# Next batch's tokens: rows serve statistics alone, a second copy laid out by feature is centred and scaled, and no row is transposed

## The chip, the cores and the metric

The kernel runs on one core of a Trainium2 chip. The metric is device time in microseconds (us) of one execution, the median of several runs.

## The reference

Input x is 4 batches of 1024 tokens by 1024 features in float32. One block of a pre-norm network is computed:

```
h   = x + attention(layernorm(x))          # 16 heads of 64, block-local window of 256 keys,
                                           # and 64 chosen query tokens per head attend to all 1024 keys
out = h + layernorm(h) @ (W_ffn * scale[:, None]).T + bias
layernorm(x) = (x - mean(x)) / sqrt(var(x) + 1e-5)     # over the 1024 features of a token
```

The chosen tokens are the first, the last, and the 62 with the largest query norm. Their rows of the attention output replace the local ones.

## The kernel before

Every fp32 matmul operand is split into a rounded high part and the rest (`_hi`, `_lo`), and three products are summed. So each product costs three matmul passes, and each operand a copy (ACT, high part) and a subtraction (DVE, low part).

`xT_hi`, `xT_lo` hold a batch's normalised tokens transposed: features on the partitions, 8 groups of 128 features by 1024 tokens. Four batches run one after another. A batch begins with a query phase: 8 slices of 128 query columns are projected, turned back to token rows, stored in memory, and their norms ranked on DVE (`top_find`, `top_rows`, first half of the heads). Then come 8 units of `attend(n, hp)`, one for each pair of heads. Within a unit PE runs the local scores in 4 steps, their transposes, the products with V, the global part, and, between these, the projection of V and K of the next pair in 8 parts (`part(0)` to `part(7)`, L648). In unit 7 these parts are the first query projections of the next batch. The order of all engines is written out by hand; every engine executes its own list in order and waits on semaphores.

**How the next batch's xT is made, before.** The rows of the next batch (for the last batch: of W_ffn, whose "norm" is the scale alone) come one tile of 128 tokens at a time into the slot of `q_store` that the unit's query has just left (`load_rows`, L236). In each unit DVE takes the moments of the tile (`row_moments`, L1066, two `bn_stats`), a chain of 14 links for 1/sqrt by Newton steps and two more for the weight case (`row_roots`, L1073), and normalises into `xn_row` (`row_normalise`, L1076). In the next unit PE transposes the tile in two halves of four 128x128 transposes (`turn_row`, L498; they stand behind `weigh(u, 0)` and `part(2)`), ACT copies each half out of PSUM (`keep_row`, L776), and in units 6 and 7, as xT comes free, ACT and DVE split the kept tiles into `xT_hi` (`row_hi`) and `xT_lo` (`row_lo`).

**SP, the DMA queue.** It issues the loads and the stores in one order. In a unit `hp`: `load_rows` (waits for `q_split`), then `stores` (L245): the next V slice of the weights into `w_raw[0]`, the outputs of steps 0 and 1 (`store_ctx`, 128 KB each), the next K slice into `w_raw[1]`, the outputs of steps 2 and 3.

**POOL.** In a unit (`unit`, L388): `split_key`, `normalise` of steps 0, 1, 2, `split_value`, `normalise` of step 3. `normalise(n, hp, s)` writes one of two output buffers and so waits until the store of step `s - 2` has landed:

```
pool.wait_ge(ctx_stored[s % 2], u * (16 * STEPS // 2) + 16 * (s // 2) + 16)     # L353
```

`split_value(n, hp)` makes `w_hi[0]`, `w_lo[0]` of the V slice of pair `hp + 2`. It waits for that slice in `w_raw[0]` and for PE's end of `part(5)`, and PE waits for it ahead of `part(0)` of unit `hp + 1` (L480).

**The K hand-over.** PE's `part(6)` of the K projection waits until the K half before it has left PSUM: ACT writes `kT_hi` (`k_hi_out`), DVE `kT_lo` (`k_lo_out`, L1125). In `attend` on DVE, `k_lo_out(n, hp + 1, 0)` stands behind `global_maxima`, `row_moments`, `pv_sums(u, 3)`, `top_norms(5)` and `split_q`.

Of the kernel before, what the change touches and what calls it, by code (L numbers as in the profile page):

```python
# [24 lines left out]
P = 128  # L25
# [13 lines left out]
MISC = 4  # L39
# [14 lines left out]
def build(nc, rows_in, wstream, bq, bk, bv, scale_ffn, bias_ffn, out):  # L54
    q_rows = nc.dram_tensor("q_rows", (SEQ * HEADS, HD), F32, kind="Internal").ap()
    ctx_rows = nc.dram_tensor("ctx_rows", (ROWS, HD), F32, kind="Internal").ap()
    idx_dram = nc.dram_tensor("idx_dram", (BATCH, 2 * HEADS * TOPK), U32, kind="Internal").ap()
# [4 lines left out]
    with ExitStack() as ctx:  # L62
# [8 lines left out]
        q_store = sb("q_store", [P, TILES + 2, SEQ])  # L71
# [14 lines left out]
        x_norm = sb("x_norm", [P, 2, HID])  # L86
        ident = sb("ident", [P, P])
        bq_c, bk_c, bv_c = sb("bq_c", [P, PAIRS]), sb("bk_c", [P, PAIRS]), sb("bv_c", [P, PAIRS])
        scale_c = sb("scale_c", [P, KC])
# [5 lines left out]
        ln_scale = sb("ln_scale", [P, 1])  # L95
        is_weight, zero_c = sb("is_weight", [P, 1], U32), sb("zero_c", [P, 1])
        norms = sb("norms", [P, TILES, HEADS])
        norm_rows = x_norm[0:HALF_HEADS, :, :]
        last_rows, xn_row = q_store[:, 0, :], q_store[:, TILES + 1, :]
        x_buf = [last_rows, xn_row]  # L100
# [19 lines left out]
        lin_c, lin_h = q_store[:, 1:3, :], q_store[:, 3:5, :]  # L120
        lin_hb, lin_o = q_store[:, 5:7, :], q_store[:, 7:9, :]
# [17 lines left out]
        rows_loaded = sem("rows_loaded")  # L139
        weight_set = sem("weight_set")  # L140
        ln_step = sem("ln_step"); xn_set = sem("xn_set")
        x_turned = sem("x_turned"); row_out = sem("row_out")
# [71 lines left out]
        def _(sp):  # L214
            for b in range(2):
                sp.sem_inc(q_stored[b], 16)
                sp.sem_inc(o_stored[b], 16)
            for t in range(TILES):
                if t >= 4:
                    sp.wait_ge(first_in[t % 4], 16)  # L220
                sp.dma_start(q_store[:, t + 1, :], rows_in[t]).then_inc(first_in[t % 4], 16)
                if t == 1:
                    for dst, src in ((bq_c, bq), (bk_c, bk), (bv_c, bv), (scale_c, scale_ffn)):
                        sp.dma_start(dst[:, :], src).then_inc(const_in, 16)
# [11 lines left out]
            def load_rows(n, hp):  # L236

                sp.wait_ge(q_split, n * PAIRS + hp + 1)
                apart(sp)
                sp.wait_ge(rows_loaded, n * (16 * TILES) + 16 * hp + 16)  # L240
                apart(sp)
                sp.dma_start(q_store[:, bass.ds(hp + 1, 1), :].rearrange("p a c -> p (a c)"),
                             rows_in[n * TILES + hp + TILES]).then_inc(rows_loaded, 16)
# [1207 lines left out]
```

## Time and profile before

| | |
|---|---|
| median of 3 runs | 2351.7 us (2348.31 to 2351.74) |
| the profiled execution | 2351.89 us |
| its span, first to last instruction | 2350.3 us |
| mean granted TensorE clock | 0.975 |
| busy: PE, DVE, ACT, POOL | 94%, 66%, 36%, 25% |
| chain that ended last | PE 72%, DVE 18%, issue 7%, ACT 2% |

The busy shares are of the span. "Granted clock" is a share of 2.4 GHz; 0.50 is 1.2 GHz. The chain is followed back from the last instruction to whatever released each step; "issue" is time in which the engine waited for nothing that the profile shows. A row of the timeline begins with its start and its duration in us, then engine, line, operation, output and inputs, a count, and in brackets the idle time ahead of it with the engine that ended it. Matmuls overlap, so the cost of a group on PE is read from its start to the next group's start.

### The profile page before, as it was taken

Reading aid. Unit: us, or ns where it says so; the run is one execution under the profiler, and the core shown is the slowest. Engines: PE = TensorE matmul, PEld = TensorE weight load, DVE = VectorE, ACT = ScalarE, POOL = GpSimd, SP = SyncE. Lnnn points to the kernel's source line nnn. Section 1 sums busy time; section 2 is a strip of 40 time slices with the busy share of each in tenths; the row PEclk is TensorE's granted clock in tenths of the full one; section 3 lists DMA queues with packets and bytes.
Section 4 is the critical chain, followed back from the end, with each engine's and each line's share of the span. In section 5 each row is a group of like instructions: output and inputs, shape, how many; then the busy total and the mean of one; then the engine's idle time right before and its main releaser. Section 6 shows DMA issues by size and latency. Waiting matters only on the chain.

```text
span 2350.3 us, 40763 instructions
## 1 busy us (share of the span) xinstructions
PE 2218.1 (94%) x13024; PEld 1879.8 (80%) x13024; DVE 1553.2 (66%) x3434; ACT 857.4 (36%) x2218; POOL 597.6 (25%) x464
## 2 busy tenths in 40 slices
PE   5999989999999899999998999999999987999999
PEld 4878878877788788777887887878887876888887
DVE  5677775664877755748777656486776666666664
ACT  2334445442254344522544355324543551000000
POOL 1231231123321221242312312423123202222221
PEclk9999999999999999999999999999999988999999
DMA  3321111103211111033111111221111103333331
GB/s 126 103 62 51 41 55 38 49 28 107 74 39 49 56 38 49 30 92 87 39 49 41 56 38 39 90 82 48 48 40 51 36 12 125 134 134 134 134 134 72
DMA packets 106170, 159.13 MB, mean 68 GB/s; under 512 B 9616, under 2 KB 75222, under 8 KB 106064
## 3 DMA queue, kind: packets, MB, share of 16 engines
q1 hardware_dynamic: 98128, 138.98, 18.2%
q10 hardware_dynamic: 4608, 16.78, 1.8%
q0 software_dynamic: 3328, 2.17, 0.4%
q8 instruction: 41, 0.67, 0.1%
q14 instruction: 65, 0.53, 0.1%
HBM read 106.48 MB, written 51.41 MB: 67 GB/s over the span
## 4 chain that ended last, share of the span: by engine, by line
PE 72%; DVE 18%; issue 7%; ACT 2%; DVEq 1%; DMA 0%; ACTq 0%; SPq 0%; another core or an unknown queue 0%
PE proj L460 32%; PE proj L742 15%; PE pv L596 7%; PE turn L586 5%; PE score L571 4%; PE pv L640 2%; PE score L621 2%; DVE x_norm L1147 2%; DVE top_idx L1145 2%; DVE top_val L1143 2%; DVE neg_max L1201 2%; PE misc L608 1%; PE misc L508 1%; PE turn L733 1%; DVE kT_lo L1128 1%
## 5 line engine op out<-in xcount | busy, mean ns | idle before, releaser
L460 PE MATMUL proj<-xT_hi,w_hi 128*128 128x512 f32 x1536 | 418.8, 416 | 51.8 <-DVE kT_lo L1128 51.8
L460 PE MATMUL proj<-xT_hi,w_lo 128*128 128x512 f32 x1536 | 413.2, 400 | 0.0
L460 PE MATMUL proj<-xT_lo,w_hi 128*128 128x512 f32 x1536 | 382.1, 391 | 0.0
L460 PEld LDWEIGHTS proj<-xT_hi,w_hi 128*128 128x128 f32 x1536 | 285.7, 196 | 119.5 <-DVE kT_lo L1128 60.9
L460 PEld LDWEIGHTS proj<-xT_lo,w_hi 128*128 128x128 f32 x1536 | 288.4, 188 | 63.3
L460 PEld LDWEIGHTS proj<-xT_hi,w_lo 128*128 128x128 f32 x1536 | 285.2, 191 | 64.4 <-issue 0.7
L864 ACT ACTIVATE probs<-score,neg_max 128x256 f32<-128x256 f32 (+1 forms) x512 | 229.2, 460 | 173.7 <-DVE neg_max L1192 101.5
L354 POOL TENSOR_TENSOR ctx_out<-pv_sum,row_inv 128x256 f32<-128x256 f32 x128 | 82.0, 641 | 755.1 <-DVE pv_sum L1229 749.1
L330 POOL CAST w_hi<-w_raw 128x1024 fp32r<-128x1024 f32 x96 | 111.9, 1166 | 544.4 <-PE proj L460 421.9
L332 POOL TENSOR_TENSOR w_lo<-w_raw,w_hi 128x1024 fp32r<-128x1024 f32 x96 | 237.5, 2474 | 7.8
L596 PE MATMUL pv<-v_nat,pT_lo 128*128 128x128 f32 x1024 | 199.1, 276 | 0.0
L596 PE MATMUL pv<-v_nat,pT_hi 128*128 128x128 f32 x1024 | 196.9, 274 | 1.6 <-DVE pT_lo L1208 1.6
L1208 DVE TENSOR_TENSOR pT_lo<-turn,pT_hi 128x512 fp32r<-128x512 f32 x256 | 165.0, 684 | 42.1 <-ACT pT_hi L877 39.5
L1229 DVE TENSOR_TENSOR pv_sum<-pv,pv_lo 128x256 f32<-128x256 f32 x128 | 54.3, 424 | 193.7 <-ACT pv_lo L888 193.7
L596 PEld LDWEIGHTS pv<-v_nat,pT_hi 128*128 128x128 f32 x1024 | 160.6, 192 | 10.1 <-DVE pv_sum L1229 1.4
L596 PEld LDWEIGHTS pv<-v_nat,pT_lo 128*128 128x128 f32 x1024 | 156.1, 193 | 0.0
L440 POOL TENSOR_TENSOR q_store<-q_store,bias_b 128x1024 f32<-128x1024 f32 x32 | 76.7, 2397 | 287.2 <-DVE q_store L1400 284.8
L877 ACT CAST pT_hi<-turn 128x512 fp32r<-128x512 f32 x256 | 138.9, 595 | 7.2 <-PE turn L586 2.4
L586 PE MATMUL turn<-ident,probs 128*128 128x128 f32 (+1 forms) x1024 | 139.0, 281 | 0.0
L844 ACT ACTIVATE kT_hi<-proj,bk_c 128x512 fp32r<-128x512 f32 x64 | 44.3, 693 | 205.7 <-PE proj L460 205.7
L586 PEld LDWEIGHTS turn<-ident,probs 128*128 128x128 f32 (+1 forms) x1024 | 117.6, 141 | 0.1
L1110 DVE TENSOR_TENSOR q_sq<-q_nat 128x512 f32<-128x512 f32 x64 | 57.1, 892 | 90.5 <-ACT q_nat L814 84.1
(147 smaller groups left out, 3652.9 us busy)
## 6 DMA issues: line engine op xcount, KB each, us to landing
w_raw<-in_wstream SPq DMA_DIRECT2D x96, 512.0 KB, 4.1
q_store<-in_rows SPq DMA_DIRECT2D x72, 512.0 KB, 3.3
q_rows<-q_nat SPq DMA_DIRECT2D x64, 256.0 KB
ctx_rows<-ctx_out SPq DMA_DIRECT2D x128, 128.0 KB, 1.8
q_store<-ctx_rows SPq DMA_DIRECT2D x32, 512.0 KB, 4.1
out<-q_store ACTq DMA_DIRECT2D x32, 512.0 KB, 2.6
bias_b<-in_bias_ffn SPq DMA_DIRECT2D x1, 512.0 KB, 8.0
idx_cols<-idx_dram POOLq DMA_DIRECT2D x32, 1.0 KB, 3.3
```

The source lines that it names most:

```text
L330: pool.tensor_copy(w_hi[b][:, :], w_raw[b][:, :]).then_inc(w_hi_set, 1)
L332: pool.tensor_tensor(w_lo[b][:, :], w_raw[b][:, :], w_hi[b][:, :].bitcast(F32), ALU.subtract).then_inc(w_split[b], 1)
L354: pool.tensor_tensor(ctx_out[:, s % 2].rearrange("p b h d -> p h b d"), pv_sum[:, s % 2].rearrange("p (h b) d -> p h b d", h=2), row_inv[: ...
L440: pool.tensor_tensor(lin_hb[:, b, :], lin_h[:, b, :], bias_b[:, :], ALU.add).then_inc(hb_set, 1)
L460: mm = pe.matmul(proj[:, bank, :], w[b][:, k * P:k * P + P], x[:, k, half * HALF:half * HALF + HALF], start=(m == 0), stop=(m == 23), skip ...
L571: mm = pe.matmul(score[:, at:at + hi - lo], qs[r, i * BLK:i * BLK + BLK], ks[r, lo:hi], start=(first and b == 0), stop=stop, skip_group_ch ...
L586: mm = pe.transpose(turn[0:rows, col:col + P], probs[:, src:src + rows], ident[:, :])
L596: mm = pe.matmul(pv[:, g * P:g * P + P], pt[:, (g * 2 + c) * P:(g * 2 + c) * P + P], v_nat[:, 2 * s + b + c, h, :], start=(m == 0), stop=( ...
L742: mm = pe.matmul(proj[:, half, :], x[b][:, k * P:k * P + P], w[:, k, half * 512:half * 512 + 512], start=(m == 0), stop=(m == 23), skip_gr ...
L864: last = act.activation(probs[:, at:at + hi - lo], score[:, at:at + hi - lo], ACT.Exp, bias=neg_max[:, g:g + 1], accum_out=row_sum[:, g:g ...
L877: act.copy(pT_hi[:, h * 512:h * 512 + 512], turn[:, h * 512:h * 512 + 512]).then_inc(pT_hi_set, 1)
L1208: dve.tensor_tensor(pT_lo[:, cols], turn[:, cols], pT_hi[:, cols].bitcast(F32), ALU.subtract).then_inc(pT_set, 1)
```

## The change

The input also comes transposed by the host (`cols_in`: for each batch 8 tiles of 128 features by 1024 tokens, and W_ffn transposed after them). Rows of the next batch are loaded for their moments alone, two tiles in each of units 0 to 3 (`x_buf`, two buffers). One chain of roots for all 8 tiles runs in unit 4. SP writes means and deviations to memory (`stat_rows`) and reads them back spread over all partitions (`mean_b`, `rstd_b`). In units 5 and 6 POOL subtracts the means from the feature tiles (`centre`), DVE multiplies by the deviations (`column_scale`), and ACT and DVE split into xT by token halves (`column_hi`, `column_lo`) in units 6 and 7. For the last batch's next "batch", W_ffn, only `column_scale` by the scale runs. `turn_row`, `keep_row`, `row_hi`, `row_lo`, `row_normalise`, `last_tile` are gone. Besides, `k_lo_out(n, hp + 1, 0)` and `k_hi_out(n, hp + 1, 0)` move ahead, `top_norms(5)` and the moments move behind the last low parts, `k_hi_out(n, 0, 0)` moves ahead of `norms_out(n, 1)`, and PE's batch loop is cut at another place.

```diff
 # tables
-        ROW_ORDER = [TILES - 1] + list(range(TILES - 1))
-        EARLY_ROWS, LATE_ROWS = (1, 2, 3, 4), (5, 6, 0)
+        COLS = list(range(KC - 3)) + [KC - 1, KC - 3, KC - 2]
+        SCALE_AT = {(5, 3): (0,), (5, 4): (1, 2), (5, 6): (3, 4), (6, 0): (5,), (6, 1): (6,), (6, 3): (7,)}
+        LO_AT = {(6, 5): (0, 1), (6, 6): (2, 3, 4, 5, 6, 7), (7, 1): (0, 1, 2), (7, 2): (3, 4, 5), (7, 3): (6, 7)}
+        HI_AT = {(6, 4): (0, 1), (6, 5): (2, 3), (6, 6): (4, 5, 6, 7), (7, 0): (0, 1, 2), (7, 1): (3, 4, 5), (7, 2): (6, 7)}
 # SP
+            def load_rows(n, j):
+                for b in range(2):
+                    if not (isinstance(j, int) and j == 0):
+                        sp.wait_ge(rows_seen, n * TILES + 2 * j + b - 1)
+                    apart(sp)
+                    sp.dma_start(x_buf[:, b, :], rows_in[n * TILES + 2 * j + b + TILES]).then_inc(rows_loaded[b], 16)
+            def spread_stats(n):
+                sp.wait_ge(stat_set, n + 1)
+                apart(sp)
+                for i, src in enumerate((ln_mv[:, :, 0], ln_rstd[:, :])):
+                    sp.dma_start(stat_rows[n, i].rearrange("(t p) -> p t", p=P), src,
+                                 allow_slow_non_contiguous=True).then_inc(stat_out, 16)
+                sp.wait_ge(stat_out, n * 32 + 32)
+                apart(sp)
+                for i, dst in enumerate((mean_b, rstd_b)):
+                    sp.dma_start(dst, stat_rows[n, i].partition_broadcast(P)).then_inc(stat_in, 16)
-                with sp.Fori(0, PAIRS - 2) as hp:
-                    load_rows(n, hp)
+                with sp.Fori(0, HALF_PAIRS - 1) as hp:
+                    load_column(n, hp)
+                    if following:
+                        load_rows(n, hp + 1)
                     stores(n, hp, [wstream[PAIRS + 4 + 2 * hp], wstream[PAIRS + 5 + 2 * hp]])
+                for hp in range(HALF_PAIRS - 1, PAIRS):
+                    if hp < KC - 1:
+                        load_column(n, hp)
+                    if hp == HALF_PAIRS:
+                        load_last_column(n, following)
+                        if not following:
+                            spread_scale(n)
+                    if hp == HALF_PAIRS + 1 and following:
+                        spread_stats(n)
...
 # POOL
+            def centre(n, ks):
+                for k in ks:
...
+                    pool.tensor_tensor(column(k), column(k), mean_b, ALU.subtract).then_inc(col_centred, 1)
+                unit(n, PAIRS - 3, cols=(COLS[0:1], COLS[1:3], COLS[3:5], COLS[5:7]) if following else ((),) * STEPS)
+                unit(n, PAIRS - 2, value=following, cols=(COLS[7:8], (), (), ()) if following else ((),) * STEPS)
 # PE, attend
                 weigh(u, 0)
-                turn_row(n, u, hp, 0)
...
                 part(2)
-                turn_row(n, u, hp, 1)
 # PE, ahead of the units
+                pe.wait_ge(norm_rows_set, n * 2 + 2)
 # ACT, attend
+                if not last:
+                    act.wait_ge(scored, u * EVENTS + EVENTS)
+                    out(1, 0)
                 global_exps(u)
                 pv_lo_out(u, 3)
-                if not last:
-                    out(1, 0)
 # DVE, attend, from the global maxima on
                 global_maxima(u)
                 if not last:
-                    row_moments(n, hp + 1, tile)
+                    k_lo_out(n, hp + 1, 0)
                 pv_sums(u, 3)
-                top_norms(5)
                 if not last:
                     split_q(u + 1, hp + 1)
-                    k_lo_out(n, hp + 1, 0)
+                columns(5)
                 gp_lo_out(u)
                 inverses(u, STEPS)
+                top_norms(5)
+                if following and hp < HALF_PAIRS:
+                    row_moments(n, hp)
+                if following and hp == HALF_PAIRS:
+                    row_roots(n)
+                columns(6)
                 if not last:
-                    row_roots(n, hp + 1, scale_c[:, bass.ds(hp, 1)])
-                    row_normalise(n, hp + 1, tile)
                     k_lo_out(n, hp + 1, 1)
                 g_out(n, u, hp)
+            def row_moments(n, j):
+                for b in range(2):
+                    dve.wait_ge(rows_loaded[b], n * (8 * TILES) + 16 * j + 16)
+                    apart(dve)
+                    moments(x_buf[:, b, :], 2 * j + b, seen=rows_seen)
```

## Rows read from the trace of the kernel before

**Rows 1.** The page, busy time of each engine.

```profile
PE 2218.1 (94%) x13024; PEld 1879.8 (80%) x13024; DVE 1553.2 (66%) x3434; ACT 857.4 (36%) x2218; POOL 597.6 (25%) x464
```

**Rows 2.** Waits of PE: waiter <- releaser, us in total, times, longest.

```profile
PE proj L460 <- DVE kT_lo L1128: 51.8, 32, 6.8
```

**Rows 3.** Timeline of PE: one marker of units 1, 2, 3, 4, 6, 7 of batch 1.

```profile
710.03 0.30 PE L614 MATMUL misc<-ident,q_pad 128*128 128x128 f32 x1
...
754.17 0.30 PE L614 MATMUL misc<-ident,q_pad 128*128 128x128 f32 x1
...
798.50 0.30 PE L614 MATMUL misc<-ident,q_pad 128*128 128x128 f32 x1
...
851.28 0.30 PE L614 MATMUL misc<-ident,q_pad 128*128 128x128 f32 x1
...
939.58 0.30 PE L614 MATMUL misc<-ident,q_pad 128*128 128x128 f32 x1
...
991.87 0.30 PE L614 MATMUL misc<-ident,q_pad 128*128 128x128 f32 x1
```

**Rows 4.** Timeline of PE, units 1 and 2 of batch 1.

```profile
701.39 0.60 PE L508 MATMUL misc<-ident,q_store 128*128 128x128 f32 x4
701.75 0.42 PE L596 MATMUL pv<-v_nat,pT_hi 128*128 128x128 f32 x2
...
721.39 2.11 PE L460 MATMUL proj<-xT_hi,w_hi 128*128 128x512 f32 x8 [0.48 <-DVE kT_lo L1128]
...
729.21 0.50 PE L571 MATMUL score<-kT_hi,qT_hi 64*128 64x192 f32 x4
...
730.48 2.07 PE L460 MATMUL proj<-xT_hi,w_hi 128*128 128x512 f32 x8
...
740.34 0.62 PE L508 MATMUL misc<-ident,q_store 128*128 128x128 f32 x4
740.80 1.04 PE L586 MATMUL turn<-ident,probs 128*128 128x128 f32 x8
```

**Rows 5.** Timeline of PE, first matmuls after long waits, batches 1 and 2.

```profile
816.19 3.78 PE L460 MATMUL proj<-xT_hi,w_hi 128*128 128x512 f32 x8 [6.82 <-DVE kT_lo L1128]
...
1109.84 3.43 PE L460 MATMUL proj<-xT_hi,w_hi 128*128 128x512 f32 x8 [3.26 <-DVE kT_lo L1128]
```

**Rows 6.** Windows after the same wait in batch 0; behind the counts stand granted clock, DMA share, GB/s.

```profile
337.90:341.50 3.60, 3.60 (x9) 2.83 (x10) 3.22 (x16) 0.00 (x0) 2.50 (x4) 0.50 0.73 261
```

**Rows 7.** Timeline of DVE: end of unit 1, batch 1; both halves' `top_rows`, one instruction.

```profile
716.61 1.28 DVE L1026 BATCH_NORM_STATS2 ln_stats<-q_store 128x6 f32<-128x512 f32 x2
...
723.50 0.15 DVE L1222 RECIPROCAL row_inv<-row_sum 128x1 f32<-128x1 f32 x1
...
809.67 2.39 DVE L1157 TENSOR_SCALAR idx_row<-idx_f,row_base 8x64 f32<-8x64 f32 x1
...
1105.89 0.24 DVE L1157 TENSOR_SCALAR idx_row<-idx_f,row_base 8x64 f32<-8x64 f32 x1
```

**Rows 8.** Timeline of POOL, unit 1 of batch 1.

```profile
711.38 0.61 POOL L354 TENSOR_TENSOR ctx_out<-pv_sum,row_inv 128x256 f32<-128x256 f32 x1 [5.92 <-DVE pv_sum L1229]
720.10 1.48 POOL L330 CAST w_hi<-w_raw 128x1024 fp32r<-128x1024 f32 x1 [8.11 <-PE proj L460]
721.65 2.40 POOL L332 TENSOR_TENSOR w_lo<-w_raw,w_hi 128x1024 fp32r<-128x1024 f32 x1
```

**Rows 9.** Timeline of SP, where unit 2 of batch 1 begins.

```profile
726.34 0.36 SPq L242 DMA_DIRECT2D q_store<-in_rows  x1
727.06 0.36 SPq L248 DMA_DIRECT2D w_raw<-in_wstream  x1
```

**Rows 10.** Source views of L248 (V slice, behind a row load) and L279 (bias, spread): landing.

```profile
DMA to landing us min/median/max: 3.6/4.5/5.0
...
DMA to landing us min/median/max: 8.0/8.0/8.0
```

**Rows 11.** Groups by line, DVE: a tensor_tensor of 128x1024 with both inputs in SBUF.

```profile
L1383 DVE TENSOR_TENSOR q_store<-q_store 128x1024 f32<-128x1024 f32 x32 | 38.9, 1217 | 0.0
```

More of the change, by code:

```diff
@@ L259, in batch @@
                 apart(sp)
-                sp.wait_ge(rows_loaded, n * (16 * TILES))
-                apart(sp)
-                sp.dma_start(last_rows, rows_in[n * TILES + 2 * TILES - 1]).then_inc(rows_loaded, 16)
+                if following:
+                    load_rows(n, 0)
                 for i in range(PAIRS):
@@ L689, in opening_q, with head @@
                 project_pair(0, 0, b, half, part)
-            def batch(n, following):
+            def head(n):
                 turn_early_q(n, 0, 0)
@@ L905, in out, with columns @@
                         k_hi_out(n, hp + 1, h)
-                def rows_hi(i):
-                    if early and i in EARLY_ROWS or last and i in LATE_ROWS:
-                        row_hi(n, i)
+                def columns(place):
+                    if early or last:
+                        for i in HI_AT.get((hp, place), ()):
+                            column_hi(n, i, int(last))
                 v_hi_out(u, 0)
                 exps(u, 0)
-                rows_hi(5)
+                columns(0)
                 v_hi_out(u, 1)
@@ L1021, in link_of, with moments, roots @@
                 return link
-            def moments(src, i, last=True):
+            def moments(src, i, last=True, seen=None):
                 for half in range(2):
                     stats = dve.bn_stats(ln_stats[:, i, half, :], src[:, half * 512:half * 512 + 512])
-                if last:
+                if seen is not None:
+                    stats.then_inc(seen, 1)
+                elif last:
                     stats.then_inc(ln_step, 1)
-            def roots(steps, size=1, weight_scale=None, at=0, between=None):
+            def roots(steps, size=1, at=0, between=None):
                 links = [1]
@@ L1245, in g_out, with attend @@
                                   row_inv[:, 4 * STEPS:4 * STEPS + 1], None, ALU.mult).then_inc(g_set, 1)
-            def attend(n, hp, half, top=(), early=False, last=False):
-                u = n * PAIRS + hp
-                tile = q_store[:, bass.ds(hp + 1, 1), :].rearrange("p a c -> p (a c)")
-                def rows_lo(i):
-                    if early and i in EARLY_ROWS or last and i not in EARLY_ROWS:
-                        row_lo(n, i)
+            def attend(n, hp, half, top=(), following=True):
+                u, last = n * PAIRS + hp, hp == PAIRS - 1
                 def top_norms(k):
@@ L1260, in top_norms, with columns @@
                             top_rows(n, 1)
+                def columns(place):
+                    for i in SCALE_AT.get((hp, place), ()):
+                        column_scale(n, i, following)
+                    for i in LO_AT.get((hp, place), ()):
+                        column_lo(n, i, int(last))
                 maxima(u, 0)
@@ L1277, in attend @@
                 top_norms(2)
[L1278 removed]
+                columns(2)
                 pv_sums(u, 1)
@@ L1362, in batch @@
                 k_lo_out(n, 0, 1)
[L1363 to L1374 removed]
+                attend(n, 0, 0, range(3, 8), following)
+                attend(n, 1, 0, range(8, 13), following)
+                attend(n, 2, 0, range(13, 18), following)
+                attend(n, 3, 0, range(18, TOP_STEPS), following)
+                for hp in range(HALF_PAIRS, PAIRS):
+                    attend(n, hp, 1, (), following)
+            with dve.Fori(0, BATCH - 1) as n:
+                batch(n, True)
+            batch(BATCH - 1, False)
             def lin_norm(t, b, turn2):
```

239 lines of the change are left out of this document (110 added, 129 removed).

## The prediction, as it was put on record

> **What bounds the kernel now.** I read the page first: PE is busy 94% of the span [rows 1], so a microsecond counts only if it comes off PE or off a wait that PE makes. The waits of PE come second. One stands out: the projection waits 32 times for DVE's kT_lo, 51.8 us in all [rows 2]. Third, the timeline of PE, by one marker in each unit. A quiet unit is 754.17 - 710.03 = 44.14 us. Unit 4 takes 851.28 - 798.50 = 52.78 and unit 7 991.87 - 939.58 = 52.29 [rows 3]. So a batch has seven unit steps at the pace of PE's own work and two that are some 8.5 us longer. In a quiet unit the only wait is one of 0.48 us ahead of part(6) [rows 4]. The long units hold a wait, and after it PE runs slowly: eight matmuls that take 2.1 us [rows 4] take 3.78 and 3.43 us after waits of 6.82 and 3.26 us [rows 5], and in such a stretch the granted clock is 0.50, that is 1.2 instead of 2.4 GHz [rows 6]. I price a wait of 3 us or more at its length plus 1.9 us (1.7 from the first eight, a little from the next).
>
> **The change, part by part.** All against the profiled execution, 2351.89 us (span 2350.3, 1.6 around it), which is within 0.2 us of the median of the runs shown.
>
> *Row transposes gone.* From their start to the next group: 701.75 - 701.39 = 0.36 and 740.80 - 740.34 = 0.46 us [rows 4], 0.82 a unit. 32 units: **-26.2**. ACT's copies and DVE's roots and normalising lay beside PE.
>
> *The wait ahead of part(6).* DVE now does k_lo_out right behind the global maxima, and ACT k_hi_out as soon as the global scores are done, 5 us before part(6). 24 quiet units: 24 x 0.48 = **-11.5**. The 6.82 us wait of unit 3 has the same cause with top_find and top_rows in front, and goes too (below). What is left of the 51.8 is 51.8 - 11.5 - 4 x 6.8 = 13.1, or 3.3 in each batch: the K half ahead of unit 0 1109.84 in [rows 5]. DVE was busy without a break there; last_tile leaves that stretch: 1.28 us of moments [rows 7], a chain of 16 dependent links and a normalising of 128x1024, together more than the wait. 4 x (3.3 + 1.5) = **-19.2**. PE's new wait for the norm rows stands later than ACT's copy ends: nothing.
>
> *Unit 3 to 4.* Before: 52.78 - (44.14 - 0.48) = 9.1 us too long. Now top_find, top_rows (2.39 - 0.24 us shorter where POOL isn't beside it) and four bn_stats (two pairs of 1.28 us, [rows 7]) stand between the last low parts, which end 38.5 us into the unit by 723.50 [rows 7], and the maxima of unit 4: some 1 us late. The gather of the second half's queries keeps POOL at the start of unit 4, and split_key, 3.9 us [rows 8], comes after it; the old 9 us covered that, and now I expect it some 1.5 us late for part(2). I take 3 us: 4 x (9.1 - 3) = **-24.4**. Bounds of what returns: 0 to 7 us.
>
> *Unit 7.* Before: 52.29 - 43.66 = 8.6 too long, from DVE's row_lo work and a late K half. The new pieces are half as long (128x512) and spread over places where the timeline has DVE and ACT idle. ACT has three copies ahead of v_hi_out(1), so I leave 1.5: 3 x 7.1 = **-21.3**, and 3 for the last batch's unit 7: **-3**.
>
> *Unit 5 and 6, the columns.* POOL gets 7 subtractions of 2.4 us (the size of 721.65 [rows 8]) in unit 5, DVE 5 multiplications of 1.2 us [rows 11]. POOL has the room: idle 5.92 and 8.11 us [rows 8]. The statistics are there in time: DVE ends the roots as unit 5 begins; two issues, a write, a spread read of two 512 KB tiles. The dearest load in the trace that is like it took 8.0 us [rows 10]; with 8 for each trip the tiles stand at 17 us into the unit, and the first place where DVE takes a column is just ahead of the third output step, whose POOL part begins at 711.38 - 685.0 = 26 [rows 8]. But DVE and POOL get in each other's way: a tensor_scalar of 8x64 takes 0.24 us at 1105.89 and took 2.39 us at 809.67 [rows 7], beside POOL's w_lo. pad_q, column_scale and split_q now meet back-to-back subtractions; turn_gq and the global exponentials wait behind. I take 3.5 us in unit 5 and 0.5 in unit 6 (bounds 0 and 10: four operations, each held 2.4): 3 x 4 = **+12**.
>
> The Trainium skill ("SBUF — State Buffer", section "SBUF: two separate sides") says that VectorE and GpSimd share one port pair by an exclusive lock, which VectorE takes in a two-port mode or with two SBUF inputs, and that the later one blocks for the whole instruction. The row of 2.39 us agrees with it for tensor_scalar. By it column_scale, with two SBUF inputs, would be held as well; by the short row alone nothing would be, and these 12 us would be 0.
>
> *SP, the part that costs.* In the new loop load_rows(n, hp + 1) stands ahead of stores(n, hp). It waits for rows_seen, which DVE gives in row_moments(n, hp), at the END of unit hp. Behind it in SP's list stand the V slice of pair hp + 2 and all four output stores of unit hp. Before, the row load waited only for q_split and the V slice followed 0.72 us later, at the unit's start [rows 9]. Follow it for units 0, 1 and 2 of the three batches with a following one, in us from the unit's start (685.0 in rows 4, 7 and 8, from 729.2 less 44.1):
> - DVE's last reciprocal: 723.50 - 685.0 = 38.5, less 0.8 for the transposes: 37.8. First tile seen at 39.1, second at 40.3 (1.28 a tile, [rows 7]).
> - SP: row loads at 39.2 and 40.5, V slice at 41.2, store of step 0 at 41.9 (0.7 apart, [rows 9]).
> - Landing: a V slice 0.72 us behind another load of 512 KB takes 4.5 [rows 10]. So the slice lands at about 45.7, and the store behind it at 46.
> - POOL stands in normalise of step 2 since about 26 (711.38 [rows 8]), because its buffer's store has not been issued. It goes on at 46.1; 0.6, then split_value with 1.1 + 2.4: done at 50.3. Before, split_value began at 720.10, 35 us into the unit, and had 6 us to spare.
> - PE needs it 1.27 us into the next unit (730.48 - 729.21 [rows 4]); the unit being 44.14 - 0.82 - 0.48 = 42.8 long, at 44.1. It waits 6.1 us, then the slow stretch: 8.0.
>
> Three times in each of three batches: 9 x 7.9 = **+71**. Bounds of one: 4 us (the store lands alone in 1 us and nothing queues) to 12.4 (each of the three 512 KB loads as slow as the 8.0 of [rows 10]).
>
> **Sum:** -26.2 - 11.5 - 19.2 - 24.4 - 21.3 - 3 + 12 + 71 = -22.6. 2351.9 - 22.6 = **2329 us**, 1% faster. The linear stage at the end is not touched.
>
> **Rivals.**
> - *The queue stall is not there* or is covered by slack that I miss. For it: POOL is only 25% busy [rows 1]. Against it: the order in SP's list and POOL's wait for the store are plain, and the slack of 6 us is less than the 11 by which the store is late. Time: 2329 - 71 = 2258. Chance 0.13 (with half-way cases to 2295).
> - *The same stall, dearer, and the whole slower than before.* Place: SP's queue at the end of units 0 to 2. If three loads of 512 KB in a row cost 4.3 us each instead of 1.5, the store lands at 51 and each stall is 12.4: 2329 + 9 x 4.5 = 2369. It turns the sign from 10.4 us a stall on. For it: the one load that took 8.0, in a crowd. Against it: every V slice behind a row landed in at most 5.0 [rows 10]. Chance 0.19.
> - *POOL and DVE in unit 5.* The lock holds all four operations, or the four-byte pieces of the statistics are slow and DVE stands in front of column_scale with everything behind it. 10 to 14 us more a batch with the slow clock: 2329 + 3 x 10 = 2359; 2345 if half of it. Chance 0.12.
> - *Only the transposes count:* all moved waits come back elsewhere and there is no stall: 2352 - 26 - 12 = 2314. It lies inside the range of the first. Chance 0.06.
>
> **How the numbers follow.** The forecast has 0.50. A difference under 0.2% (4.7 us) can't be told from no change. My own case gives 2305 to 2350, nearly all faster: 0.46 faster, 0.03 within, 0.01 slower. No stall and transposes alone: 0.19 faster. The dearer stall: 0.02 faster, 0.03 within, 0.14 slower. Unit 5: 0.03, 0.03, 0.06. Together 0.70, 0.09, 0.21. The range for 8 in 10 is 2288 to 2366: it leaves out most of the first rival and the far end of the second.
>
> **What would show it.** Right: the ctx stores of units 0, 1, 2 in batches 0 to 2 are issued in one burst behind the row loads at the unit's end, POOL idles some 19 us ahead of its third normalise, and PE's largest wait is "L460 <- POOL w_lo", nine times about 6 us, with units 1, 2, 3 near 51 us; the last batch has units of 42.8. kT_lo no longer appears in PE's waits. Wrong: units 1 to 3 at 43 (no stall), or over 53; more than 10 us lost in unit 5; a wait on the statistics.

## The result, and the profile after

The changed kernel takes 2362.2 us (median of 5 runs, 2358.95 to 2366.78), the one before 2349.8 (5 runs). The ratio is 1.0053, 95% interval 1.0038 to 1.0068: slower by 0.5%. The forecast was 2329 us and faster. The profiled run took 2358.95 us, its span is 2357.4 (before 2350.3), its mean granted clock 0.969 (before 0.975). "The changed kernel" is here always the one of the diff.

The page after, busy time of each engine:

```profile
PE 2186.3 (93%) x12768; PEld 1857.1 (79%) x12768; DVE 1494.4 (63%) x2965; ACT 827.3 (35%) x2186; POOL 652.2 (28%) x488
```

PE has 32 us less work than in [rows 1], and the span is 7 us longer: PE now waits more. Waits of PE after (waiter <- releaser, us in total, times, longest):

```profile
PE proj L525 <- POOL w_lo L383: 84.3, 15, 7.8
...
PE proj L525 <- DVE xT_lo L1148: 9.1, 3, 3.0
...
PE proj L525 <- DVE kT_lo L1172: 5.4, 4, 1.4
```

The 51.8 us for kT_lo [rows 2] are down to 5.4, all ahead of unit 0. In their place stands w_lo with 84.3, of which nine waits of 7.0 to 7.8 us make 67. Where, the markers tell: the timeline of PE after, the same marker as in [rows 3], all of batch 1 (units 0 to 7):

```profile
672.32 0.30 PE L666 MATMUL misc<-ident,q_pad 128*128 128x128 f32 x1
724.59 0.30 PE L666 MATMUL misc<-ident,q_pad 128*128 128x128 f32 x1
776.78 0.30 PE L666 MATMUL misc<-ident,q_pad 128*128 128x128 f32 x1
828.23 0.30 PE L666 MATMUL misc<-ident,q_pad 128*128 128x128 f32 x1
874.40 0.30 PE L666 MATMUL misc<-ident,q_pad 128*128 128x128 f32 x1
917.39 0.30 PE L666 MATMUL misc<-ident,q_pad 128*128 128x128 f32 x1 [0.38 <-DVE q_pad L1279]
965.24 0.30 PE L666 MATMUL misc<-ident,q_pad 128*128 128x128 f32 x1
1012.60 0.30 PE L666 MATMUL misc<-ident,q_pad 128*128 128x128 f32 x1
```

"The step of unit 3" below is from the marker of unit 2 to that of unit 3. The steps here are 52.3, 52.2, 51.5 (units 1 to 3), 46.2, 43.0, 47.9, 47.4 (4 to 7). In the last batch, which has no rows to load, six of them are 42.5 or less, and that of unit 4 is 52.0. So the nine long steps lie where the prediction put the queue's stall. The steps of unit 4, of units 5 and 6, and of unit 7 are also longer than it had them.

One stall, read through the timelines of SP, DVE, POOL and PE:

```profile
738.12 2.45 DVE L1071 BATCH_NORM_STATS2 ln_stats<-x_buf 128x6 f32<-128x512 f32 x4
739.62 1.53 SPq L248 DMA_DIRECT2D x_buf<-in_rows  x2
741.49 0.33 SPq L286 DMA_DIRECT2D w_raw<-in_wstream  x1
742.23 1.11 SPq L239 DMA_DIRECT2D ctx_rows<-ctx_out  x2
743.54 0.49 SPq L291 DMA_DIRECT2D w_raw<-in_wstream  x1
...
748.21 0.61 POOL L405 TENSOR_TENSOR ctx_out<-pv_sum,row_inv 128x256 f32<-128x256 f32 x1 [28.18 <-DMA ctx_rows<-ctx_out]
...
749.89 2.34 POOL L383 TENSOR_TENSOR w_lo<-w_raw,w_hi 128x1024 fp32r<-128x1024 f32 x1
...
752.28 3.78 PE L525 MATMUL proj<-xT_hi,w_hi 128*128 128x512 f32 x8 [7.78 <-POOL w_lo L383]
```

DVE frees the two row buffers, SP issues two row loads, the V slice, two stores and the K slice in 4.4 us, the first store lands 6.0 us after its issue (742.23 to 748.21), and POOL's third normalise, split_value and PE follow one behind the other. Windows of that time (PE, PEld, DVE, ACT, POOL busy, granted clock, DMA share, GB/s):

```profile
744.70:748.30 3.60, 0.00 (x0) 0.00 (x0) 2.77 (x7) 2.19 (x10) 0.09 (x1) 1.00 0.93 322
...
752.30:756.10 3.80, 3.80 (x9) 3.03 (x10) 0.00 (x0) 0.00 (x0) 3.72 (x3) 0.51 0.29 73
```

While PE waits, the DMA engines are 0.93 busy: three 512 KB loads were issued ahead of the store (two row tiles, the V slice) and one behind it (the K slice). After the wait PE runs at a granted clock of 0.51, 1.2 GHz.

### The profile page after: what moved, and what is told of

Its sections match the earlier page's. It is cut to its first block, busy times and chain, and to the rows that moved or that the text cites. A ratio compares the mean times of both kernels' runs of the same rounds, so it can differ in the third digit from the quotient of the medians.

```text
span 2357.4 us, 38561 instructions
## 1 busy us (share of the span) xinstructions
PE 2186.3 (93%) x12768; PEld 1857.1 (79%) x12768; DVE 1494.4 (63%) x2965; ACT 827.3 (35%) x2186; POOL 652.2 (28%) x488
## 4 chain that ended last, share of the span: by engine, by line
PE 64%; DVE 14%; issue 14%; POOL 3%; DMA 2%; ACT 2%; DVEq 0%; POOLq 0%; SPq 0%; ACTq 0%
PE proj L525 28%; PE proj L798 15%; PE pv L648 8%; PE turn L638 4%; PE score L623 3%; DVE x_norm L1191 2%; DVE top_idx L1189 2%; DVE top_val L1187 2%; DVE q_sq L1154 2%; POOL w_lo L383 1%; DVE q_store L1133 1%; PE turn L789 1%; PE score L673 1%; PE pv L692 1%; DVE norms L1156 1%
## 5 line engine op out<-in xcount | busy, mean ns | idle before, releaser
L525 PE MATMUL proj<-xT_hi,w_hi 128*128 128x512 f32 x1536 | 424.5, 421 | 98.8 <-POOL w_lo L383 84.3
L383 POOL TENSOR_TENSOR w_lo<-w_raw,w_hi 128x1024 fp32r<-128x1024 f32 x96 | 230.6, 2402 | 7.8
L648 PE MATMUL pv<-v_nat,pT_hi 128*128 128x128 f32 x1024 | 196.3, 274 | 1.7 <-DVE pT_lo L1252 1.7
L1221 DVE TENSOR_TENSOR v_nat<-misc,v_nat 64x256 fp32r<-64x256 f32 (+3 forms) x128 | 55.1, 449 | 169.8 <-ACT v_nat L897 169.8
L1154 DVE TENSOR_TENSOR q_sq<-q_nat 128x512 f32<-128x512 f32 x64 | 73.1, 1142 | 106.3 <-ACT q_nat L861 103.0
L891 ACT ACTIVATE kT_hi<-proj,bk_c 128x512 fp32r<-128x512 f32 x64 | 44.2, 690 | 252.9 <-PE proj L525 153.9
```

What stands on the lines that cost most here:

```text
L383: pool.tensor_tensor(w_lo[b][:, :], w_raw[b][:, :], w_hi[b][:, :].bitcast(F32), ALU.subtract).then_inc(w_split[b], 1)
L525: mm = pe.matmul(proj[:, bank, :], w[b][:, k * P:k * P + P], x[:, k, half * HALF:half * HALF + HALF], start=(m == 0), stop=(m == 23), skip ...
L648: mm = pe.matmul(pv[:, g * P:g * P + P], pt[:, (g * 2 + c) * P:(g * 2 + c) * P + P], v_nat[:, 2 * s + b + c, h, :], start=(m == 0), stop=( ...
L1154: dve.tensor_tensor(q_sq[:, :], src, src, ALU.mult).then_inc(q_squared[h], 1)
```

## The experiments

Each ratio is to the kernel before, run on the same chip in the same session. In the expectations of runs 1 to 4, Theory 1 is the prediction's queue stall.

**1. The stores ahead of the row loads.**

```diff
                     load_column(n, hp)
-                    if following:
-                        load_rows(n, hp + 1)
                     stores(n, hp, [wstream[PAIRS + 4 + 2 * hp], wstream[PAIRS + 5 + 2 * hp]])
+                    if following:
+                        load_rows(n, hp + 1)
```

> The changed kernel, with one thing different: in SP's loop over units 0 to 2 load_rows(n, hp + 1) stands behind stores(n, hp) instead of ahead of it. Theory 1 (SP's list: the store of step 0 waits behind the row load, POOL waits for that store, PE for POOL's split_value): the nine waits of PE for w_lo of 7.0 to 7.8 us at the start of units 1, 2, 3 go, those units fall from 52.2 to 42.5 us, and the time falls by 9 x 9.7 = 87 us, from 2362 to 2275, well under the kernel before (2350). Theory 2 (the longer time comes from the added DMA traffic, 175 MB against 159, which slows the loads wherever they stand): the waits stay or move, and the gain is under 20 us. Theory 3 (the loss comes from units 4 to 7 of each batch): no change in units 1 to 3, gain near 0.

Measured: 2276.5 us (2272.2 to 2281.2), ratio 0.9692 [0.9675, 0.9709]. Markers of units 1 and 2 of batch 1 on PE, and its wait for w_lo in the last batch:

```profile
688.71 0.30 PE L666 MATMUL misc<-ident,q_pad 128*128 128x128 f32 x1
731.16 0.30 PE L666 MATMUL misc<-ident,q_pad 128*128 128x128 f32 x1
...
1728.66 3.78 PE L525 MATMUL proj<-xT_hi,w_hi 128*128 128x512 f32 x8 [7.35 <-POOL w_lo L383]
```

All nine long steps are 42.4 or 42.5 us. The queue's order costs 2362.2 - 2276.5 = 86 us, 9.5 a stall; the nine steps by themselves are 87.9 us shorter, 9.8 each. Everything else in the change brings 72 us, not the 94 of the forecast. Both halves of the missed sum are in this one run. The long wait in the last batch's unit 4 is untouched and so has another cause.

**2. The moments earlier, the queue as changed.**

```diff
+                if following and hp < HALF_PAIRS:
+                    row_moments(n, hp)
                 columns(3)
...
-                if following and hp < HALF_PAIRS:
-                    row_moments(n, hp)
```

> The changed kernel with SP's list as it is, but DVE takes the moments of the next tiles behind pad_q, at about 22 us into the unit, instead of at its end. Theory 1: SP is released at 25 us, the store of step 0 lands before 30, POOL's third normalise is a few us late and split_value not at all. The nine waits go without any change of SP's order or of the traffic: 2362 - 87 = 2275, plus up to 1 us in each of 12 units, because 2.5 us of bn_stats meet an idle time of 1.7 to 2.2 us on DVE there: 2275 to 2287. Theory 2 (traffic): the same bytes, no gain. A rival to Theory 1 within the queue: that the waits come from the place of the loads (three of 512 KB in a row) and not from their waiting; then they shrink by half at most, 2320.

Measured: 2287.5 us (2283.7 to 2290.0), ratio 0.9749 [0.9733, 0.9765]; units 1 to 3 take 42.4. So the stall ends from either side, the order of SP's list or the event that it waits for. Its step of unit 4 sums to 201.6 us over the four batches against 196.3 in run 1. That is 5 of the 11 us between the medians; the rest I have not located. The two profiled spans don't help, they differ by 2.5 us: run 1's is of its slowest execution, this one's of its fastest.

**3. The V slice alone ahead of the row loads, and 4. two stores alone.** Which of the queued things makes the stall?

```diff
 # slice_ahead, in batches with a following one
                     load_column(n, hp)
+                        sp.wait_ge(w_split[0], n * BUFS + PAIRS // 2 + 3 + hp)
+                        sp.dma_start(w_raw[0][:, :], wstream[PAIRS + 4 + 2 * hp]).then_inc(raw_in[0], 16)
                         load_rows(n, hp + 1)
+                        store_ctx(n, hp, 0)
...
 # two_stores_ahead
                     load_column(n, hp)
+                        store_ctx(n, hp, 0)
+                        store_ctx(n, hp, 1)
                         load_rows(n, hp + 1)
+                        sp.wait_ge(w_split[0], n * BUFS + PAIRS // 2 + 3 + hp)
...
```

> The changed kernel with one thing of the queue moved: in units 0 to 2 of the batches with a following one, SP issues the V slice of the weights ahead of the row loads, at the unit's start; the four output stores stay behind them. Theory 1 (one queue in order, POOL's third normalise waits for the store of step 0, which lands some 6 us after the first row load is issued, and split_value comes only after it): the V slice being early gives little. With one 512 KB load less ahead of it the store is issued 0.7 us earlier and lands 1 to 2 us earlier, so each of the nine waits for w_lo falls from 7.5 to 5 or 6 us, units 1 to 3 take 50 to 51 us instead of 52.2, and the whole comes out at 2338 to 2350 us. Rival A (the stall is the V slice's late landing, the stores don't matter): the waits vanish and the time is that of the kernel with all of it ahead, 2276 us. Rival B (what costs is the crowd of four 512 KB transfers, not the order): halfway, near 2310 us.

> The changed kernel with the other thing of the queue moved: in units 0 to 2 of the batches with a following one, SP issues the stores of output steps 0 and 1 ahead of the row loads; the V slice, the K slice and the stores of steps 2 and 3 stay behind them. Theory 1 (both queued things hold split_value): POOL's third normalise is no longer late (no wait for the store near 28 us), but split_value still needs the V slice, which is issued about 41 us into the unit and lands 4.5 us later, with 3.5 us of split behind it: waits of 4.5 to 5.5 us instead of 7.5, nine times, units 1 to 3 at 49.5 to 50.5 us, and the whole near 2335 us (2328 to 2345). If the store alone were the cause: 2276 us. If this kernel and the one with the V slice ahead each keep more than half of the stall while both moved together lose all of it, the two waits lie one behind the other, nearly equally late.

Measured: V slice ahead 2355.4 us (2350.8 to 2365.4, 10 runs), ratio 1.0031 [1.0017, 1.0046]; two stores ahead 2360.4 (2355.9 to 2364.3, 6 runs), ratio 1.0047 [1.0033, 1.0062]. Timelines with the V slice ahead:

```profile
733.17 1.51 SPq L248 DMA_DIRECT2D x_buf<-in_rows  x2
735.11 1.11 SPq L239 DMA_DIRECT2D ctx_rows<-ctx_out  x2
...
739.72 0.61 POOL L414 TENSOR_TENSOR ctx_out<-pv_sum,row_inv 128x256 f32<-128x256 f32 x1 [26.16 <-DMA ctx_rows<-ctx_out]
...
743.79 3.78 PE L534 MATMUL proj<-xT_hi,w_hi 128*128 128x512 f32 x8 [5.75 <-POOL w_lo L392]
```

And with two stores ahead:

```profile
742.50 0.33 SPq L315 DMA_DIRECT2D w_raw<-in_wstream  x1
...
748.41 1.04 POOL L390 CAST w_hi<-w_raw 128x1024 fp32r<-128x1024 f32 x1 [20.88 <-DMA w_raw<-in_wstream]
...
751.92 3.76 PE L534 MATMUL proj<-xT_hi,w_hi 128*128 128x512 f32 x8 [6.43 <-POOL w_lo L392]
```

Each alone keeps nearly all of the stall: the nine waits average 5.7 and 6.7 us, where the changed kernel has 7.5. POOL needs the store and the slice, both stand behind the row loads, and whichever remains lands almost as late: in the rows above the store 4.6 us after its issue, the slice 5.9. The second wait was hidden behind the first, which rules out that the slice alone, or the store alone, is the cause. With one of the loads out of the crowd the store lands 1.4 us sooner (4.6 instead of 6.0), a first sign of what the crowd costs. Both runs were slower than expected (2338 to 2350 and 2328 to 2345), and not for the same reason. With two stores ahead the waits themselves were longer than the expected 4.5 to 5.5: I had counted the slice's landing at 4.5 us when it took 5.2 to 6.4. With the V slice ahead the waits and steps came as expected (5.4 to 6.1 us, 50.0 to 51.7), and the nine steps are 12.3 us shorter in sum than in the changed kernel; but the steps of unit 4 and of units 5 and 6 took 3.0 and 5.8 us more, and the cause of that stays open.

**5. Before, with the K hand-over alone.**

```diff
                 global_maxima(u)
                 if not last:
+                    k_lo_out(n, hp + 1, 0)
                     row_moments(n, hp + 1, tile)
                 pv_sums(u, 3)
-                top_norms(5)
                 if not last:
                     split_q(u + 1, hp + 1)
-                    k_lo_out(n, hp + 1, 0)
                 rows_lo(3)
                 gp_lo_out(u)
                 inverses(u, STEPS)
+                top_norms(5)
 # and on ACT out(1, 0) ahead of global_exps(u), as in the change
```

> The kernel before with the earlier K hand-over of the change alone: k_lo_out(n, hp + 1, 0) directly behind global_maxima, k_hi_out(n, hp + 1, 0) as soon as the global scores are done, top_norms(5) behind the last low parts. Row transposes and row statistics stay. If the waits of PE for kT_lo are what I took them for: 24 x 0.48 = 11.5 us go, and the 6.82 us wait of unit 3 with its slow stretch (9.1 us in each batch) gives way to a smaller one, since top_find, top_rows, roots and normalising now all stand ahead of k_lo_out(n, 4, 1): 2350 - 11.5 - 4 x 3 = 2326. The rival, that PE's order is bounded elsewhere and the waits only move: 2350.

Measured: 2310.8 us (2309.3 to 2313.6), ratio 0.9848 [0.9832, 0.9865]; 15 us less than the 2326 expected. A quiet step is 43.4 us (0.7 to 0.8 shorter, where the 0.48 us wait had been counted) and the step of unit 4 is 47.2 to 49.1 instead of 52.8 to 53.6. Over the four batches that is 21.8 us, as much as unit 4 gains in the whole change (21.2). Moving two copies ahead and top_norms(5) back brings half of what the whole change brings without its stall (37 of 72 us).

**6. Before, with a quarter of the row transposes.**

```diff
-                for k in range(KC // 2):
+                for k in range(1):
                     mm = pe.transpose(misc[:, k * P:k * P + P], xn_row[:, c:c + P], ident[:, :])
```

> The kernel before, with each half of a row tile turned by one transpose instead of four; three quarters of the next batch's tokens are left out of xT. It weighs the row transposes on PE by themselves. If they lie on the path at their start-to-start time, 0.82 us a unit: 26.2 x 3/4 = 19.7 us less, 2330. If PE has to wait there for something else anyway: no change, 2350.

This kernel leaves out three quarters of the next batch's xT. Measured: 2325.3 us (2321.7 to 2328.8), ratio 0.9911 [0.9891, 0.9930]: 23 us, 0.71 for each unit's six transposes, so 0.95 for all eight against 0.82 in the sum. The price of the first term was sound.

**7. The last column's load and the scale's behind the stores of unit 4**, on top of run 1.

```diff
                     if hp < PAIRS - 2:
                         stores(n, hp, [wstream[PAIRS + 4 + 2 * hp], wstream[PAIRS + 5 + 2 * hp]])
+                        if hp == HALF_PAIRS:
+                            load_last_column(n, following)
+                            if not following:
+                                spread_scale(n)
```

> stores_first, and the load of the last feature tile (and, in the last batch, of the spread scale) moved behind the stores of unit 4. Asked: why unit 4 of the last batch alone is 51.9 us long, with 7.4 us of waiting for w_lo, where the other batches have 2.5 to 3.1. Theory 1: SP puts four loads of 512 KB (two of them extra) on the DMA engines just before POOL stores the indices of the chosen tokens; the gather waits for that small store, split_key for the gather, PE for split_key. Then the wait falls to 3 or less and unit 4 to 45 to 47 us: 5 to 7 us less, 2270 against 2276. Rival: POOL's own list (gather ahead of split_key) is the whole cause: no change.

Measured: 2274.7 us (2273.2 to 2278.8), ratio 0.9689 [0.9674, 0.9704]. As a whole not to be told from run 1. The last batch's step of unit 4 fell from 51.9 to 47.9 us and PE's wait there from 7.35 to 3.88: the way that Theory 1 had it, but less (it had 45 to 47 us, and a wait of 3 or less). Timelines of the changed kernel there:

```profile
1782.62 0.36 SPq L256 DMA_DIRECT2D q_store<-in_cols  x1
1783.03 0.45 SPq L264 DMA_DIRECT2D x_buf<-in_cols  x1
1784.17 0.34 SPq L281 DMA_DIRECT2D x_norm<-in_scale_ffn  x1
1784.55 0.43 SPq L286 DMA_DIRECT2D w_raw<-in_wstream  x1
...
1785.06 0.65 POOL L416 DMA_DIRECT2D idx_dram<-idx_out  x1 [3.02 <-DVE idx_out L1211]
1792.01 1.90 POOL L425 DMA_DIRECT2D idx_cols<-idx_dram  x3 [6.30 <-DMA idx_dram<-idx_out]
...
1806.59 3.78 PE L525 MATMUL proj<-xT_hi,w_hi 128*128 128x512 f32 x8 [7.55 <-POOL w_lo L383]
```

The same two places in run 7:

```profile
1709.46 1.90 POOL L425 DMA_DIRECT2D idx_cols<-idx_dram  x3 [2.65 <-DMA idx_dram<-idx_out]
...
1724.02 1.22 PE L525 MATMUL proj<-xT_hi,w_hi 128*128 128x512 f32 x2 [3.88 <-POOL w_lo L383]
```

POOL's store of a few indices is not in SP's list, yet POOL waited 6.30 us for it behind SP's four 512 KB loads (6.14 in run 1), and 2.65 in run 7, where only two loads were ahead of it, issued 2.0 and 2.4 us before. PE's wait fell by as much, 3.5 us from run 1 to run 7. The Trainium skill ("DMA: Bandwidth & Descriptors", section "Rules for kernel authors") says that DMAs issued by different engines run on the same 16 DMA engines and interleave; these two waits agree.

**8. No subtraction on POOL**, on top of run 7; the means are left out.

```diff
-                    pool.tensor_tensor(column(k), column(k), mean_b, ALU.subtract).then_inc(col_centred, 1)
+                    pool.sem_inc(col_centred, 1)
```

> stores_late with the subtraction of the means on POOL left out (POOL waits and signals as before), so DVE multiplies uncentred columns. Everything else of units 5 and 6 stays: the same DVE work, the same DMAs, the same waits for the statistics. Theory 1 (POOL and DVE hold each other up while both read SBUF): DVE's column_scale falls from 6.26 and 5.37 us for two to 2.4, q_pad from 3.07 to 0.36, the waits for exponentials (2.0) and v_nat (3.2) in units 5 and 6 go: the 7.5 us that these two units are too long in each of three batches go, 22 us, 2270 to 2248. Theory 2 (DVE simply has five multiplications too many for unit 5): at most 5 us. Unit 7 with its 3.0 us wait for xT_lo should stay as it is by both.

**9. The subtraction on DVE**, just ahead of the multiplication, on top of run 7. Besides, POOL's list loses `centre`, and the tiles are spread over more places of units 5 and 6 (`SCALE_AT`).

```diff
+                if following:
+                    dve.tensor_tensor(column(k), column(k), mean_b, ALU.subtract).then_inc(col_centred, 1)
+                    dve.wait_ge(col_centred, n * KC + i + 1)
                 dve.tensor_tensor(column(k), column(k), rstd_b, ALU.mult).then_inc(col_scaled, 1)
```

> stores_late with the means subtracted by DVE instead of POOL, spread over units 5 and 6: eight more instructions of 1.2 us for DVE in each of three batches, none for POOL. Theory 1 (the lock): units 5 and 6 lose most of their 7.5 us in spite of 9.8 us more DVE work; 2270 - 3 x 5 = 2255. Theory 2 (DVE's amount of work): slower than stores_late, 2275 to 2285.

Measured: 2251.8 us (2249.4 to 2254.5), ratio 0.9584 [0.9569, 0.9598] without it, 2262.5 (2260.9 to 2269.6), ratio 0.9639 [0.9622, 0.9655] on DVE. Against run 7 the first is 23 us, 7.6 a batch: that is what POOL's subtractions cost in all. Timelines of the changed kernel in units 5 and 6 of batch 1:

```profile
912.46 4.73 POOL L449 TENSOR_TENSOR q_store<-q_store,x_norm 128x1024 f32<-128x1024 f32 x2
914.18 3.07 DVE L1279 TENSOR_SCALAR q_pad<-q_sel 64x64 f32<-64x64 f32 x2
919.67 5.74 POOL L449 TENSOR_TENSOR q_store<-q_store,x_norm 128x1024 f32<-128x1024 f32 x2
920.23 6.26 DVE L1133 TENSOR_TENSOR q_store<-q_store,x_norm 128x1024 f32<-128x1024 f32 x2
...
945.25 0.63 PE L660 MATMUL misc<-ident,vT 128*128 128x128 f32 x4 [3.21 <-DVE v_nat L1221]
...
962.57 0.36 DVE L1279 TENSOR_SCALAR q_pad<-q_sel 64x64 f32<-64x64 f32 x2
```

The second of the two subtractions and of the two multiplications that start at 919.67 and 920.23, each by itself:

```profile
922.04 3.37 POOL L449 TENSOR_TENSOR q_store<-q_store,x_norm 128x1024 f32<-128x1024 f32 x1
...
923.08 3.40 DVE L1133 TENSOR_TENSOR q_store<-q_store,x_norm 128x1024 f32<-128x1024 f32 x1
```

And of DVE in run 8:

```profile
859.00 2.33 DVE L1133 TENSOR_TENSOR q_store<-q_store,x_norm 128x1024 f32<-128x1024 f32 x2
```

Two multiplications take 2.33 us alone and 6.26 beside two subtractions; the pair of q_pad 0.36 alone and 3.07 beside them. PE waits for what stands behind on DVE. In run 8 the steps of units 5 and 6 are 42.4 us, all six. In run 9 they keep 3.9 us a batch, all in the step of unit 6: there DVE's doubled work still meets POOL's weight splits (one multiplication takes 3.29 us beside a w_lo of 3.24), which my 2255 us left out. The Trainium skill ("SBUF — State Buffer", section "SBUF: two separate sides") says that a VectorE operation with two SBUF inputs and a GpSimd operation that reads SBUF exclude each other for a whole instruction. These rows agree: the two engines take turns. The first multiplication ends at 923.16, 1.1 us after POOL's first subtraction (922.08), the second at 926.48, 1.1 us after POOL's second (925.41), and one alone takes 1.2. POOL's second subtraction in turn takes 3.37 instead of 2.4. No single operation of DVE in this trace is held for two of POOL's instructions.

**10. The best version found.** Run 9, with some high and low parts of xT and four of the multiplications one place or more earlier in unit 6, and unit 4's split_key ahead of the gather.

```diff
-        LO_AT = {(6, 5): (0, 1), (6, 6): (2, 3, 4, 5, 6, 7), ...
+        LO_AT = {(6, 4): (0, 1, 2, 3), (6, 6): (4, 5, 6, 7), ...
-        HI_AT = {(6, 4): (0, 1), (6, 5): (2, 3), (6, 6): (4, 5, 6, 7), ...
+        HI_AT = {(6, 4): (0, 1, 2, 3), (6, 5): (4, 5), (6, 6): (6, 7), ...
 # POOL
+                split_key(n, HALF_PAIRS)
                 store_rows(n, 1)
                 load_columns(n, 1)
                 gather(n, 1)
                 apart(pool)
-                unit(n, HALF_PAIRS)
+                unit(n, HALF_PAIRS, key=False)
```

> All mends together: stores ahead of row loads, last column late, centring on DVE, four of the low parts of the first token half moved ahead of POOL's split_value in unit 6, and POOL's split_key of unit 4 ahead of the gather. If the waits named are each what they look like: unit 4 falls to 43 to 44 us in all four batches (from 47 to 52), units 5 and 6 to 43, unit 7 loses its 3.0 us wait for xT_lo with its slow stretch (47.4 to 43.5). 2276 - 4 x 4.5 - 6 - 3 x 5 - 3 x 4 = 2225 at best, 2235 expected. If the waits only move on: 2255 or more.

Measured: 2242.2 us (2241.9 to 2244.6, 5 runs), ratio 0.9546 [0.9533, 0.9559]. It beats both kernels: 4.5% faster than before; 2235 us had been expected. The markers of units 6 and 7 of batch 1, 42.5 us apart, and the largest entry of the units in PE's waits:

```profile
898.92 0.30 PE L667 MATMUL misc<-ident,q_pad 128*128 128x128 f32 x1
941.38 0.30 PE L667 MATMUL misc<-ident,q_pad 128*128 128x128 f32 x1
...
PE misc L661 <- DVE v_nat L1222: 21.8, 8, 3.6
```

The wait for xT_lo is gone from unit 7, and that for w_lo is down to 2.1 us in 2. Split_key ahead of the gather paid in the last batch alone, where the step of unit 4 fell from 47.8 to 42.4 us. In the other three it is 46.2 to 48.9 (run 9: 47.4 to 47.9): PE no longer waits for w_lo there but 3.6 us for DVE's v_nat. DVE's list has the four bn_stats of unit 3 just ahead (2.5 us), which the last batch has not; that they are the cause is not tested. The step of unit 6 keeps a wait of 2.7 us for v_nat in the same batches.

## Why the prediction was wrong

The mechanism that it called the part that costs is there, in the place and the order given. The sum failed by size: all the large misses are to the same side. Step lengths of all 32 units of both profiled runs, against the forecast's terms (the transposes and the 0.48 us wait spread over the steps that they belong to):

| steps | forecast, us | measured, us | off |
|---|---|---|---|
| first step of each batch (4) | -24.4 | -24.0 | +0.4 |
| units 1 to 3, batches 0 to 2 (9) | +59.3 | +72.0 | +12.7 |
| unit 4 (4) | -27.7 | -21.2 | +6.5 |
| units 5 and 6, batches 0 to 2 (6) | +4.2 | +9.8 | +5.6 |
| unit 7, batches 0 to 2 (3) | -23.8 | -14.5 | +9.3 |
| the rest of the last batch (6) | -10.3 | -11.9 | -1.6 |
| sum | -22.7 | +10.2 | +32.9 |

What follows the last marker is 3.1 us shorter than before, which makes the +7.1 of the span. The median of the changed kernel lies another 3.2 us above its profiled execution. No single line turns the sign; the first and largest that failed is **the 71 us of "SP, the part that costs"**: it measured 86 us by run 1, 88 by the nine steps over quiet ones of 42.4. With 88 in its place and all else as forecast the sum would still be 6 us faster. Units 4 to 7 add 21 us, and the quiet steps and the end of the program, shorter than forecast, take back 9.

*Row transposes, wait ahead of part(6).* Right, a little small: a quiet unit is 42.4 us where 42.8 was forecast. Runs 5 and 6 show both terms by themselves.

*K half ahead of unit 0.* Right: 1.4 us of the wait is left, and the first steps are shorter by what was said.

*The stall.* Follow batch 1's unit 1. It starts at 699.24 - 7.00 - 1.27 = 690.97 (its own first wait is 7.00 us), and its own stall takes some 9.3 of it (7.00 and 2.3 for the slow stretch, an estimate from the nine steps below). On the unit's clock without that stall DVE ends the last reciprocal at 37.9 (forecast 37.8), SP issues the V slice at 41.2 (41.2) and the first store at 42.0 (41.9), and PE wants w_lo at 44.2 (44.1). All of this held to 0.1 us. What failed is the landing, the slice "at about 45.7, and the store behind it at 46": the slice came 6.3 us after its issue, at 47.5, and POOL went on behind the store at 47.9. I had taken the V slice behind one other 512 KB load [rows 10]; here two row loads stood ahead and the K slice followed, and the source views of the changed kernel, L239 (all stores of outputs, 128 KB) and L286 (V slices), have:

```profile
DMA to landing us min/median/max: 1.8/1.8/5.9
...
DMA to landing us min/median/max: 3.5/4.7/6.8
```

So the wait is 7.8 us instead of 6.1 here and 7.5 on average over the nine, and the slow stretch behind it costs 2.3 where 1.9 was counted (52.2 - 42.4 = 9.8, less 7.5). The rival "the same stall, dearer" had the direction right, by this mechanism; its 12.4 was too much, and doesn't follow from its own landing at 51 either, which is 5 us late and gives 12.9. But the point from which it decides, 10.4 us a stall, rested on the other terms, and with them as they came it was 72 / 9 = 8.0.

*Unit 4.* The gain itself was there, and by run 5 the K hand-over alone brings it. Forecast 3 us left over, measured 3.4 to 5.1 in the first three batches and 9.5 in the last. Split_key behind the gather was as described (PE waits 2.5 to 2.8 us). The last batch's crowd ahead of the index store was missed: the two loads that the change adds there, last column and scale, are in its diff, and I counted them at nothing; run 7 takes 3.9 us of the 9.5 off.

*Unit 7.* Forecast 1.5 us left over, measured 5.0. I had said that the smaller pieces "spread over places where the timeline has DVE and ACT idle" and did not look at POOL there. Timelines of POOL, DVE and PE in the changed kernel:

```profile
975.77 4.34 DVE L1148 TENSOR_TENSOR xT_lo<-q_store,xT_hi 128x512 fp32r<-128x512 f32 x2
976.84 2.73 POOL L383 TENSOR_TENSOR w_lo<-w_raw,w_hi 128x1024 fp32r<-128x1024 f32 x1
981.44 4.89 DVE L1148 TENSOR_TENSOR xT_lo<-q_store,xT_hi 128x512 fp32r<-128x512 f32 x3
...
986.25 0.68 DVE L1148 TENSOR_TENSOR xT_lo<-x_buf,xT_hi 128x512 fp32r<-128x512 f32 x1
988.38 3.53 PE L525 MATMUL proj<-xT_hi,w_hi 128*128 128x512 f32 x8 [3.01 <-DVE xT_lo L1148]
```

A low part takes 0.68 us, but two took 4.34 and three 4.89 beside POOL's splits, and PE waited 3.01 us for the last, again with a slow stretch. Alone the five would take some 3.4 us (5 x 0.68) instead of 9.2, so the time lost is more than PE's wait. It is the contention that the forecast priced in units 5 and 6 alone. Run 10, with the low parts in other places, has steps of 42.4 us in unit 7; it changed more than that, so the cause rests on these rows and that run agrees with it; no run takes the contention away in unit 7 alone.

*Units 5 and 6.* Forecast 4 us a batch, measured 5.7 to 8.4 over quiet units of 42.4; run 8 takes all of it away. The operations are held by one POOL instruction each, as it assumed, and what it mis-sized is what PE makes of it: in the step of unit 6 PE waits 3.4 to 5.4 us in all (in batch 1 0.38, 1.79 and 3.21, just the 5.4 by which that step is too long, at a granted clock of 1.00 behind the longest). Batches 0 and 2 have some 2 and 3 us more, and there the granted clock behind one of the waits is 0.68 and 0.50.

*The rivals.* "The stall is not there" fell. Its time of 2258 is what the sum gave without the stall; run 1 measured that kernel at 2276, and the 18 us between lie in units 4 to 7. The dearer unit 5 had the direction right too, but 10 to 14 us a batch was too much (1.7 to 4.4). "Only the transposes count" fell: run 5 gains 37 us without touching them.

*Two slips that change nothing.* The opening counts seven unit steps a batch at PE's pace and two long ones; a batch has eight units, and the sum rightly takes six quiet ones (24 x 0.48). And one stall is worked out as 8.0 us and summed as 7.9.

## What to carry to other kernels

Behind an instruction that waits, in a queue that runs in order, leave only what nobody downstream needs soon; whoever needs two of the queued things waits for the later, so each alone moved back frees almost nothing (runs 3 and 4), and both together free it all. Price a transfer by its landing in the crowd that it will stand in (here 6.0 us against 1.8 for the same store), not by its landing in the kernel before. When small gains are summed against one large loss, look at every engine that shares something with each moved operation. Here three terms were too good by 21 us: unit 7 by 9.3, for POOL's weight splits, which were in the trace of before; units 5 and 6 by 5.6, for POOL's subtractions; unit 4 by 6.5, of which one crowd of loads in the last batch is 3.9.

## What the runs showed of the hardware beyond that

A 128x512 low part on DVE, 0.68 us alone, and a 64x64 tensor_scalar, 0.18 us alone, are both held for microseconds beside POOL's 128x1024 operations with two inputs (the second of a pair of low parts took 2.89 us, of a pair of tensor_scalars 2.32); POOL's own are stretched less (one takes 2.38 us alone and 3.39 at most). The two writes of 1024 four-byte statistics laid out by partition, issued at 892.44 and 892.99 of batch 1, kept SP waiting 9.6 us; nothing on PE hung on it.
